# Softmax row sums of an attention kernel: exp(-ln x) and a Newton step in place of the VectorE reciprocal

## What is computed

```python
scores = jnp.einsum('bthd,bshd->bhts', q, k) * scale          # 16 heads, 1024 x 1024, causal
probs  = jax.nn.softmax(scores, axis=-1)
out    = jnp.einsum('bhts,bshd->bthd', probs, v).reshape(b, t, H * D)
return out @ wo
```

## Time and profile before

| | us |
|---|---|
| three runs | 1288.48, 1288.75, 1288.90 |
| median | 1288.75 |
| profiled execution, first to last instruction (its span) | 1286.1 |
| PE busy / DVE busy / POOL busy / ACT busy, whole span | 1223.4 / 905.4 / 674.5 / 589.7 |
| stretch 134 to 820 us of `attend` (686 us): PE / DVE / POOL / ACT busy | 666.9 / 581.1 / 473.1 / 351.7 |

### The profile page before, as it was taken

How to read it: one execution, slowest core, us unless ns; L and a number is a source line. 1 busy time by engine, 2 the same in 40 slices (tenths; PEclk the granted TensorE clock), 3 DMA queues, 4 the chain that set the end, 5 groups by cost and what they waited for, 6 DMA issues and landing times. The chain is left out here.

```text
span 1286.1 us, 20218 instructions
## 1 busy us (share of the span) xinstructions
PE 1223.4 (95%) x5904; PEld 806.2 (63%) x5952; DVE 905.4 (70%) x1410; ACT 589.7 (46%) x1192; POOL 674.5 (52%) x546
## 2 busy tenths in 40 slices
PE   5898899999999999999999999998999999999997
PEld 3555455555555555555555555546788887888886
DVE  6679878879888888888888798764544445444444
ACT  3453535545545445455355365453433333333332
POOL 1176766677677667676676676652233332323332
PEclk9999999999999999999999999998999999999999
DMA  5001001001000000000100001015633333433332
GB/s 200 33 1 33 1 1 33 1 1 32 0 0 15 16 0 13 18 0 0 32 0 0 15 0 58 1 26 147 180 114 114 114 114 100 134 114 114 114 114 90
DMA packets 26442, 67.33 MB, mean 52 GB/s; under 512 B 3044, under 2 KB 9700, under 8 KB 26408
## 3 DMA queue, kind: packets, MB, share of 16 engines
q1 hardware_dynamic: 26264, 66.84, 17.2%
q10 hardware_dynamic: 144, 0.07, 0.0%
HBM read 62.42 MB, written 4.47 MB: 52 GB/s over the span
## 5 line engine op out<-in xcount | busy, mean ns | idle before, releaser
L734 ACT ACTIVATE ring<-ps_s 128x512 f32<-128x512 f32 (+3 forms) x320 | 146.5, 468 | 309.3 <-PE ps_s L601 308.4
L1333 POOL TENSOR_TENSOR hl<-hf,hh 128x512 fp32r<-128x512 f32 x96 | 123.4, 1286 | 288.9 <-ACT hh L1270 288.9
L897 DVE TENSOR_REDUCE nm<-ps_m 128x1 f32<-128x512 f32 (+3 forms) x370 | 196.4, 549 | 46.0 <-PE ps_m L569 39.1
L1060 POOL TENSOR_TENSOR first<-first,ring 128x512 f32<-128x512 f32 (+3 forms) x160 | 161.2, 1007 | 89.6 <-ACT ring L734 57.1
L908 DVE TENSOR_TENSOR first<-first,ring 128x512 f32<-128x512 f32 (+3 forms) x160 | 140.6, 879 | 10.1 <-ACT ring L734 5.1
L1029 POOL TENSOR_TENSOR xtf<-xtf,sinv 128x512 f32<-128x512 f32 x62 | 79.6, 1284 | 119.1 <-DVE xtf L851 119.1
L1302 DVE TENSOR_TENSOR gs<-gs,routing 128x512 f32<-128x512 f32 x64 | 44.3, 692 | 137.8 <-ACT gs L1266 137.8
L613 PE MATMUL ps_o<-ring,kvn 128*64 128x512 f32 (+3 forms) x640 | 132.4, 493 | 0.0
L1270 ACT ACTIVATE hh<-hf 128x512 fp32r<-128x512 f32 x96 | 60.7, 633 | 121.1 <-DVE hf L1307 121.1
L1266 ACT ACTIVATE gs<-ps_g 128x512 f32<-128x512 f32 x96 | 57.4, 598 | 121.3 <-PE ps_g L1225 121.3
L913 DVE RECIPROCAL rec<-ps_x 128x512 f32<-128x512 f32 x32 | 107.3, 3352 | 4.8 <-PE ps_x L634 4.0
(11 more groups left out here) (241 smaller groups left out, 3097.1 us busy)
## 6 DMA issues: line engine op xcount, KB each, us to landing
routing<-wT_scratch SPq DMA_DIRECT2D x34, 256.0 KB, 3.7
raw_a<-in_e SPq DMA_DIRECT2D x17, 384.0 KB, 3.0
cosv<-in_e SPq DMA_DIRECT2D x17, 384.0 KB, 3.0
sinv<-wT_scratch SPq DMA_DIRECT2D x17, 384.0 KB, 3.6
raw<-in_e SPq DMA_DIRECT2D x17, 384.0 KB, 3.0
routing<-wT_scratch SPq DMA_DIRECT2D x16, 384.0 KB, 3.3
raw_a<-in_a SPq DMA_DIRECT2D x8, 512.0 KB, 3.3
raw_b<-in_b SPq DMA_DIRECT2D x8, 480.0 KB, 3.9
```

The lines of the kernel that those rows point to most:

```text
L734: nc.scalar.activation(probs(k, e), ps_s[(2 * k + e) % 3][:, off:], ACT.Exp, scale=SCALE).then_inc(exp_done, 1)
L897: nc.vector.tensor_reduce(out=to, in_=bank[:, 0:keys], axis=AXX, op=ALU.max, negate=True).then_inc(piece_max, 1)
L1060: nc.gpsimd.tensor_tensor(first[:, c, 1, off:], first[:, c, 1, off:], probs(k, 1), ALU.add).then_inc(sum_pool, 1)
L1333: nc.gpsimd.tensor_tensor(hl[:, c, :], hf[:, c, :], hh[:, c, :].bitcast(F32), ALU.subtract).then_inc(h_lo, 1)
```

## The change

The reciprocal on DVE goes. In its place:

- ACT, `guess_reciprocal`: `rec` = Ln of the sums in PSUM, then, after a wait for that on its own semaphore, `rec` = Exp(-`rec`). For Lp it stands in step 2 behind the second exponential, for L0 in step 5 between the two exponentials.
- DVE, `check_reciprocal`: `checked` = sums x `rec`. Lp: step 3. L0: step 5, behind `add_probs`.
- POOL, `scale_out`: `on` = `oe` x `rec`. Lp: step 2, behind `add_probs`. L0: step 5, behind `add_probs` and ahead of `rope_low`.
- DVE, `normalise`: `on` = (2 - `checked`) x `on`. Lp: step 4. L0: step 5, straight behind `check_reciprocal`, and it waits for POOL (`o_scaled`).
- `rec_done`, which frees the bank of the sums, is now set by `check_reciprocal`.
- ACT loads the table set `natural_log_exp_and_others` at the start of the block; before, a table was loaded ahead of the first exponential.

The core of the diff:

```diff
@@ ACT
+            def guess_reciprocal(n, x, s, c):
+                act.wait_ge(misc_ready, n + 1)
+                ge(act, on_done, s * 2 + c)
+                nc.scalar.activation(rec[:, :], ps_x[x][:, :], ACT.Ln).then_inc(ln_done, 1)
+                act.wait_ge(ln_done, s * 2 + c + 1)
+                nc.scalar.activation(rec[:, :], rec[:, :], ACT.Exp, scale=-1.0).then_inc(guess_done, 1)
...
                         exponent(s, k, 0)
+                        if k == 5:
+                            guess_reciprocal(*misc(i, b, "L0"), s, 0)
...
                         exponent(s, k, 1)
+                        if k == 2 and earlier:
+                            guess_reciprocal(*misc(i, b, "Lp"), s - 1, 1)
...
+            nc.scalar.preload_act_table_set("natural_log_exp_and_others")
...
             copy_out(s, 1)
+            n = BEFORE_LAST + len(LAST)
+            guess_reciprocal(n, n % 2, s, 1)
             out_hi(s, 1, BEFORE_LAST + len(LAST) - 1)
@@ DVE
-            def normalise(n, x, s, c):
+            def check_reciprocal(n, x, s, c):
                 dve.wait_ge(misc_ready, n + 1)
-                ge(dve, on_done, s * 2 + c)
-                nc.vector.reciprocal(rec[:, :], ps_x[x][:, :]).then_inc(rec_done, 1)
+                dve.wait_ge(guess_done, s * 2 + c + 1)
+                nc.vector.tensor_tensor(checked[:, :], ps_x[x][:, :], rec[:, :], ALU.mult).then_inc(rec_done, 1)
+
+            def normalise(s, c):
                 dve.wait_ge(rec_done, s * 2 + c + 1)
-                dve.wait_ge(o_copied, s * 2 + c + 1)
-                ge(dve, olo_done, s * 2 + c)
-                nc.vector.tensor_tensor(on[:, :], oe[:, :], rec[:, :], ALU.mult).then_inc(on_done, 1)
+                dve.wait_ge(o_scaled, s * 2 + c + 1)
+                nc.vector.scalar_tensor_tensor(on[:, :], checked[:, :], 2.0, on[:, :], ALU.subtract, ALU.mult, reverse0=True).then_inc(on_done, 1)
...
-                        if k == 2 and earlier:
-                            normalise(*misc(i, b, "Lp"), s - 1, 1)
+                        if k == 3 and earlier:
+                            check_reciprocal(*misc(i, b, "Lp"), s - 1, 1)
+                        if k == 4 and earlier:
+                            normalise(s - 1, 1)
...
-                        if k == 4:
-                            normalise(*misc(i, b, "L0"), s, 0)
+                        if k == 5:
+                            check_reciprocal(*misc(i, b, "L0"), s, 0)
+                            normalise(s, 0)
...
-            normalise(n, n % 2, s, 1)
+            check_reciprocal(n, n % 2, s, 1)
+            normalise(s, 1)
@@ POOL
+            def scale_out(s, c):
+                pool.wait_ge(guess_done, s * 2 + c + 1)
+                pool.wait_ge(o_copied, s * 2 + c + 1)
+                ge(pool, olo_done, s * 2 + c)
+                nc.gpsimd.tensor_tensor(on[:, :], oe[:, :], rec[:, :], ALU.mult).then_inc(o_scaled, 1)
...
                     for k in range(1, TPC):
                         add_probs(s, k)
+                        if k == 2 and earlier:
+                            scale_out(s - 1, 1)
...
                     for k in range(TPC + 1, STEPS):
                         add_probs(s, k)
+                        if k == 5:
+                            scale_out(s, 0)
...
             pairs_loop(pool, body)
+            scale_out(2 * PAIRS - 1, 1)
```

More of the change, by code:

```diff
@@ L412, in attend @@
         sh = keep["xtf"][:, :, :].rearrange("p k (g c) -> p (k g) c", c=CH)
-        t1, first, ring, shift, oe, rec, on, ohi, olo = tensors(nc, ctx, [
+        t1, first, ring, shift, oe, rec, checked, on, ohi, olo = tensors(nc, ctx, [
             ("t1", [P, 4, CH], F32), ("first", [P, 2, 2, CH], F32), ("ring", [P, RING, 2, CH], F32),
-            ("shift", [P, 2, 2, CH], BF16), ("oe", [P, CH], F32), ("rec", [P, CH], F32), ("on", [P, CH], F32),
+            ("shift", [P, 2, 2, CH], BF16), ("oe", [P, CH], F32), ("rec", [P, CH], F32), ("checked", [P, CH], F32), ("on", [P, CH], F32),
             ("ohi", [P, CH], F32R), ("olo", [P, CH], F32R)])
@@ L437, in attend @@
         sum_pool, sum_dve = sem("sum_pool"), sem("sum_dve")
+        ln_done, guess_done, o_scaled = sem("ln_done"), sem("guess_done"), sem("o_scaled")
         o_copied, rec_done, on_done, ohi_done, olo_done, y_added = (sem("o_copied"), sem("rec_done"), sem("on_done"),
```

## The result

| | before | after |
|---|---|---|
| median (4 runs each, side by side), us | 1288.83 (1288.48 to 1290.17) | 1314.64 (1312.78 to 1317.85) |
| ratio, 95% interval | 1 | 1.0197 (1.0181 to 1.0213) |
| profiled execution, its time | | 1315.76 |
| profiled execution, span | 1286.1 | 1313.8 |
| granted clock, mean of the span | 0.989 | 0.981 |

The account below looks back on a forecast made before the run. PE has almost no air and hangs on DVE's second maximum of steps 5 and 6. Span 1286.1 + 22.0 (15 stages x 1.47) - 0.6 = 1307.5, plus 2.65 around it: 1310 us, range 1293 to 1328.

Parts of the forecast that it names:

- The place that decides: Piece 3 on PE in step 6 waits for DVE's second maximum, then at 458.24; only that start counts.
- The chain on ACT and POOL: Step 5: Ln and Exp delay the second exponential, then POOL's addition, `scale_out` and `rope_low`; second maximum at 459.71.
- The unknown operation: DVE's three-input last product, absent from the trace: 0.69 us free to about 1.9 queued behind POOL; taken as queued.
- Rival 2: DVE wins the race or its product needs no turn with POOL: +7 us, 1296 us; chance 16%.
- DVE loses the race: Step 5: `rope_low` starts on POOL before DVE's last product, which waits for its first instruction and needs 0.55 us more.
- The size, 1.47 x 15 = 22.0: The second maximum starts 1.47 us later in each of 15 stages, +22.0 us.
- rival 1: Relief of DVE reaches PE, all three PE losses in the stage go: 16 us and the end, 1272 us; chance 6%.
- Lp costs nothing of its own: Steps 2 to 4: ACT's 1.2 us and POOL's 1.3 us for Lp are covered by waits, no cost.
- The end, -0.6: After the last stage nothing runs beside the chain: 4.08 us becomes 3.43, -0.6 us.
- Rival 4: Each Ln and Exp comes with table loads of 1.28 us on ACT: 1350 us; chance 2%.
- the clock: TensorE's clock falling after a PE wait: about 3 us for one more fall, in rival 3, not in the sum.
- rival 3: More is late: slower Ln or Exp, DVE's addition losing its turn, or a clock fall; 1317 to 1328 us; chance 17%.

Follow-up runs that it names:

- e12: Kernel before with three extra DVE maxima into an unused tile ahead of the second maximum of step 5; 1313.88 us, ratio 1.0202.
- e4: Changed kernel with POOL waiting, behind `scale_out` of L0, until DVE's last product is done; 1292.64 us, ratio 1.0029 to before.
- e10: Changed kernel with L0's `checked` written into the PSUM bank of the sums, so the last product has one PSUM operand; 1293.55 us, ratio 1.0027 to before.
- e2: Only Lp takes the new way, L0 keeps the old reciprocal on DVE; 1285.23 us, ratio 0.9975 to before.
- e8: Changed kernel with DVE's last product of L0 moved from step 5 to the start of step 7; 1279.83 us, ratio 0.9928 to before.
- e9: Changed kernel with the edits of e4 and e5 together; 1286.59 us, ratio 0.9972 to before.
- e11: Changed kernel with L0's guess behind the second exponential, `checked` in PSUM, last product in step 6 behind its second maximum; 1288.22 us, ratio 1.0002 to before.
- e6: Kernel before with two extra ACT copies into an unused tile between the two exponentials of step 5; 1291.02 us, ratio 1.0017.
- e7: Changed kernel without DVE's last product of L0 and Lp, POOL's result taken as it is; 1274.19 us, ratio 0.9895 to before.
- e3: Changed kernel with DVE's last product of L0 moved to the end of step 6; 1298.12 us, ratio 1.0078 to before.
- e5: Changed kernel with L0's guess (Ln, Exp) behind the second exponential of step 5 on ACT; 1302.51 us, ratio 1.0098 to before.
- e1: Only L0 takes the new way, Lp keeps the old reciprocal on DVE; 1329.35 us, ratio 1.0316 to before.

## Why the prediction was right, and where it was off

1310 us (1293 to 1328) was forecast, with slower at 0.88; 1314.64 was measured.

- **The place that decides** (the third of the earlier trace rows, the start of the second maximum): right. e12 shows it without the change, and so does the constant 22.5 us between date and stage length in the six kernels where PE waits for it.
- **The chain on ACT and POOL**: right, to 0.04 us at every step. Forecast behind the stage's first exponential / measured: second exponential ends 23.23 / 23.19; POOL's addition 23.32 / 23.34; `scale_out` 24.55 / 24.58; `rope_low` 25.78 / 25.81; last product ends 27.61 / 27.62; second maximum 27.53 / 27.55.
- **The unknown operation**: bounded by 0.69 free and about 1.9 queued, taken as queued. It took 1.64 and ended at 472.94, 0.55 us behind `rope_low`'s first instruction (471.13 + 1.26 = 472.39). Free it takes 0.69 (tail, e4, e10). Rival 2, at 16%, is the time that e10 and e4 give (1293.55 and 1292.64, its estimate 1296), and what it would have needed is now known: an operand in PSUM, or POOL held back. The rule of the Trainium skill that was cited ("SBUF — State Buffer", "Who interferes with whom") held, for this operation too, which reads two tiles and a constant.
- **DVE loses the race**: right. `rope_low` started 0.17 us ahead of the product (471.13 and 471.30).
- **The size, 1.47 x 15 = 22.0**: 1.44 to 1.50 in twelve stages as forecast, but 20.5 in all. The forecast took stage 7 for all 15. In stage 0, which has no Lp to normalise, the maximum stood at 23.53 before and stands at 26.31 now, 2.8 us later; and in stage 1 it came 1.28 earlier, because DVE's routing work stood ahead of it there; that is the forecast's rival 1 in one stage of 15. The rows hinted at it: the longest wait of PE for a maximum, 2.9 us, and the fall of the clock both lie in stage 1.
- **Lp costs nothing of its own**: right; that QL1 comes earlier was in the chain as 0.24 us, and e2 shows it alone as 0.21 per stage.
- **The end, -0.6**: -0.7. From the start of Ln to the end of the last product it is 896.98 + 0.69 - 894.27 = 3.40 us (forecast 3.43, before 4.08):

```profile
894.27 0.60 ACT L778 ACTIVATE rec<-ps_x 128x512 f32<-128x512 f32 x1 [0.76 <-PE ps_x L709]
894.90 0.63 ACT L780 ACTIVATE rec<-rec 128x512 f32<-128x512 f32 x1
...
895.61 1.27 POOL L1088 TENSOR_TENSOR on<-oe,rec 128x512 f32<-128x512 f32 x1 [2.67 <-ACT rec L780]
...
896.98 0.69 DVE L934 SCALAR_TENSOR_TENSOR on<-checked,on 128x512 f32<-128x512 f32 x1 [0.65 <-POOL on L1088]
```

- **Rival 4** (table loads): fell, Ln and Exp are 0.60 and 0.63 with nothing between.
- **The term that was mis-sized is the clock.** It stood in rival 3 with 3 us for one more fall and at zero in the sum. From stage 1 on there were six falls that cost 1.3 to 1.6 us each, against one longer one before: net 6.3 us. The span was forecast at 1307.5 and is 1313.8, 6.3 more: 6.3 for the clock, 1.1 ahead of stage 0 and 0.6 in the last stage, less 1.5 for the dates and 0.1 at the end. That the sum came within 5 us of the median is therefore partly two misses in opposite directions. The rows showed one fall behind a long wait of PE, and the forecast put a wait of 1.5 to 2 us into each of 15 stages; it should have carried a term for several falls, though nothing in the rows could have sized it.

## What to carry to other kernels

Before taking work off an engine, find the one date that the bottleneck hangs on and ask only whether that date moves: here 89 us less on VectorE made 26 us more, since the new path went ACT, POOL, DVE in a row ahead of it. Look at every stage that differs from the typical one: in stage 1, where VectorE had 4 us of other work ahead of that date, the same change was a gain. Where VectorE and GpSimd both read SBUF, each instruction is priced by what the other is doing when it starts; so an instruction moved by half a microsecond, or one that is itself free, changes the price of its neighbours. Put the last link of a split computation where nobody waits behind it (e8: two steps later, same instructions, 35 us less than the changed kernel), or give it an operand in PSUM.

## What the runs showed of the hardware

- Two SBUF operands against one in PSUM: the same three-input product of 128x512 beside a running GpSimd instruction takes 1.64 and 0.69 us, and GpSimd's pair 2.95 and 2.64. With two SBUF operands, whoever starts first keeps the way, even if by 0.01 us (e9: GpSimd 1.84 instead of 1.29). A cast of 128x384 with only one SBUF input pays as well: 0.37 us in the mean in e8, 1.22 in e11, where it starts 0.12 us behind a GpSimd addition.
- More work on ScalarE ahead of GpSimd can make VectorE earlier: e6, 1.85 us.
- Short falls of TensorE's clock, 3.4 us at the lower level each, behind waits of PE that come once or twice per stage. How many of the 13 stages from the third on held one, in the profiled execution of each kernel, by the longest steady wait: up to 0.7 us: 0 (before, e2, e7, e8, e9); 1.0 to 1.3: 0 (e4, e6, e10), 1 (e3, e11); 1.55 to 1.67: 1 (e5); 1.82 to 1.84: 1 (e12); 2.0 to 2.1: 5 (changed kernel) and 12 (e1). Longer waits go with more falls, but what decides in which stage one falls, and why e1 has so many more than the changed kernel behind the same waits, is open.
